# Projecting tiles 2 to 4 with split operands in a fused attention and recurrent-gate kernel

## The reference

```python
x = x + xattn(layernorm(x), ctx, ctx) @ W_proj.T + b_proj
def step(c, xt):                       # xt: rows of layernorm(x), 8 steps
    f = sigmoid(xt @ wf.T + c @ uf.T + bf)
    i = sigmoid(xt @ wi.T + c @ ui.T + bi)
    g = tanh(xt @ wc.T + c @ uc.T + bc)
    return f * c + i * g
h = tanh(layernorm(x) @ wo.T + c_final @ uo.T + bo)
return x + h
```

## Time and profile before

| | |
|---|---|
| median of three runs | 939.13 us (938.74 to 941.21) |
| profiled execution, its own time | 940.45 us |
| its span, first to last instruction | 938.5 us |
| PE busy | 920.8 us, 98% |
| DVE busy | 673.8 us, 72% |
| ACT busy | 476.1 us, 51% |
| POOL busy | 206.1 us, 22% |
| granted clock of PE | 1.000 of full speed |

### The profile page before, as it was taken

How to read it: one execution, slowest core, us unless ns; L and a number is a source line. 1 busy time by engine, 2 the same in 40 slices (tenths; PEclk the granted TensorE clock), 3 DMA queues, 4 the chain that set the end, 5 groups by cost and what they waited for, 6 DMA issues and landing times.

```text
span 938.5 us, 21983 instructions
## 1 busy us (share of the span) xinstructions
PE 920.8 (98%) x7842; PEld 716.7 (76%) x7842; DVE 673.8 (72%) x2275; ACT 476.1 (51%) x1430; POOL 206.1 (22%) x236
## 2 busy tenths in 40 slices
PE   8999899999999999999999999999999999999998
PEld 5555567678877788887877888788877888888887
DVE  6888898888779977997799878987798531143222
ACT  6888666655555544554465555555655421131222
POOL 4575322211110111111111111111101100003444
PEclk9999999999999999999999999999999999999999
DMA  9564223224443543444544444434333150049862
GB/s 299 167 191 154 86 80 109 73 82 130 132 130 116 133 131 94 139 111 126 129 141 116 117 114 123 114 108 110 98 98 92 50 164 0 1 175 383 317 235 101
DMA packets 139348, 123.58 MB, mean 132 GB/s; under 512 B 46824, under 2 KB 104168, under 8 KB 137704
## 3 DMA queue, kind: packets, MB, share of 16 engines
q1 hardware_dynamic: 138520, 121.91, 42.7%
q10 hardware_dynamic: 720, 0.27, 0.2%
HBM read 87.70 MB, written 34.46 MB: 130 GB/s over the span
## 4 chain that ended last, share of the span: by engine, by line
PE 87%; DVE 6%; issue 3%; ACT 2%; DMA 1%; POOL 0%; SPq 0%; DVEq 0%; POOLq 0%; ACTq 0%
PE ps_g L699 18%; PE ps_g L701 17%; PE ps_g L700 17%; PE ps_a L746 5%; PE ps_a L768 5%; PE ps_m L699 3%; PE ps_v L789 3%; PE ps_m L701 3%; PE ps_m L700 3%; PE ps_m L821 2%; PE ps_a L701 2%; PE ps_a L700 2%; PE ps_a L699 2%; DVE probs L1028 2%; PE ps_v L794 2%
## 5 line engine op out<-in xcount | busy, mean ns | idle before, releaser
L916 ACT ACTIVATE probs<-probs,rowmin 128x192 f32<-128x192 f32 (+1 forms) x512 | 239.4, 470 | 114.2 <-DVE rowmin L1028 114.2
L1028 DVE CUSTOM_DVE_ANT_0 probs<-ps_a,mask 128x192 f32<-128x192 f32 (+1 forms) x512 | 166.0, 385 | 30.2 <-PE ps_a L746 29.4
L699 PE MATMUL ps_g<-state_hi,gate_w 128*128 128x512 f32 x336 | 133.6, 398 | 0.0
L701 PE MATMUL ps_g<-state_hi,gate_w 128*128 128x512 f32 x336 | 131.1, 390 | 0.0
L700 PE MATMUL ps_g<-state_lo,gate_w 128*128 128x512 f32 x336 | 130.9, 389 | 0.0
L1063 DVE STREAM_TRANSPOSE keys<-probs 32x128 f32<-32x128 f32 x420 | 125.6, 299 | 5.6 <-issue 0.3
L963 ACT ACTIVATE gate<-ps_g,bias 128x512 f32<-128x512 f32 x84 | 57.6, 686 | 105.4 <-PE ps_g L701 104.8
L916 ACT ACTIVATION_READ_ACCUMULATOR probs<-probs,rowmin 128x1 f32 x512 | 96.3, 188 | 0.0
L678 POOL TENSOR_TENSOR attn_lo<-recip,attn_hi 128x512 fp32r<-128x512 f32 x23 | 29.7, 1293 | 276.4 <-ACT attn_hi L929 276.4
L921 ACT ACTIVATE probs_t<-ps_a 128x512 f32<-128x512 f32 x108 | 59.3, 595 | 50.9 <-PE ps_a L768 50.9
L699 PE MATMUL ps_g<-x2t_even,gate_w 128*128 128x512 f32 x192 | 80.0, 417 | 0.0
(11 more groups left out here) (220 smaller groups left out, 1724.9 us busy)
## 6 DMA issues: line engine op xcount, KB each, us to landing
values<-ctx_rows SPq DMA_DIRECT2D x34, 256.0 KB, 4.4
xr<-x SPq DMA_DIRECT2D x32, 256.0 KB, 3.5
keys<-ctx_t SPq DMA_DIRECT2D x16, 512.0 KB, 4.3
x_dram<-xr SPq DMA_DIRECT2D x32, 256.0 KB, 2.4
gate_w<-x2t_dram SPq DMA_DIRECT2D x8, 1024.0 KB, 9.7
keys<-ctx_t SPq DMA_DIRECT2D x16, 384.0 KB, 3.5
x2t_dram<-x2t_even SPq DMA_DIRECT2D x12, 512.0 KB, 4.1
x2t_dram<-x2t_odd SPq DMA_DIRECT2D x12, 512.0 KB, 4.4
```

What stands on the lines that cost most here:

```text
L699: pe.matmul(ps, lhs[0], rhs[0], start=start, stop=False)
L701: return pe.matmul(ps, lhs[1], rhs[0], start=False, stop=stop)
L916: act.activation(row, row, ACT.Exp, bias=rowmin[:, i % 2, h:h + 1], scale=-1.0, accum_out=rowsum[:, i // G % 2, i % G, h:h + 1]).then_inc( ...
L1028: dve.tensor_tensor_reduce(probs[:, i % 2, h, 0:SEEN[t]], ps_a[h][:, score_at[i]:score_at[i] + SEEN[t]], mask[:, MASK0[t]:MASK0[t] + SEEN[ ...
```

## The change

`WHOLE` becomes 2: tiles 2 to 4 are projected with split operands as well. Their steps `halves` are thereby in the list, at the end of slots 11, 15 and 19, right behind `mult`. The projections of tiles 2 and 3 stand behind the values of slots 12 and 16, where they stood in front; those of tiles 0 and 1 stay in front, and that of tile 4 was behind already. `split_proj` moves from slots 19 and 20 to slots 6 and 7. The waits that count from `WHOLE` (of `ln1b`, of `halves`, of the blend that overwrites `wp`) follow.

```diff
     FIRST_CELL = G * TT + 3
+    SPLIT_PROJ = G + 2
     OWN_BANKS = FIRST_CELL + 1
 
-    WHOLE = OWN_BANKS // G
+    WHOLE = 2
...
-        if s == 3 and i >= WHOLE:
+        if s == 3 and not early:
             tile_steps("mult", i)
-        if early:
+        if early and (s > 0 or i - 1 < WHOLE):
             tile_steps(("proj", "query", "turn2", "spread")[s], (i - 1, i + 1, i - 1, i)[s])
+        elif early:
+            pass
         elif n + 1 < SLOTS:
             steps.append(("exp", n + 1))
...
         if n in row_at:
             steps.append(("row", row_at[n]))
+        if early and s == 0 and i - 1 >= WHOLE:
+            tile_steps("proj", i - 1)
         gates()
...
-        if FIRST_CELL <= n < FIRST_CELL + 2:
-            steps.append(("split_proj", PAIR * (n - FIRST_CELL)))
+        if SPLIT_PROJ <= n < SPLIT_PROJ + 2:
+            steps.append(("split_proj", PAIR * (n - SPLIT_PROJ)))
```

## The result

The changed kernel takes 947.44 us (median of four runs, 945.92 to 948.40), the kernel before 940.17 beside it: ratio 1.0077, 95% interval 1.0063 to 1.0091. It is slower by 7.3 us, or 5.9 to 8.6. The forecast was 941.6 us with a range up to 944.2, so it had the direction right but not the size.

The account below looks back on a forecast made before the run. PE was taken to bound the early slots, ACT and DVE close behind. +0.5 (weights' split), +0.62, +0.62 and +0.75 (tiles 2 to 4) made +2.5 us: 942.95 profiled, 941.6 us as median, range 938.0 to 944.2.

Parts of the forecast that it names:

- The projection's own cost: PE, tiles 2 to 4: a split projection takes 2.86 us against 3.60 whole, 2.2 us less over three tiles.
- The chain of hand-overs: DVE's product through ACT's rounding and POOL's subtraction to PE: 2.22 us; net +0.62 us each for tiles 2 and 3.
- Tile 4: Slot 20: projection stays behind the values, its first product waits for the hand-overs; +0.75 us.
- The weights' split: Moved to slots 6 and 7: ACT copies delay PE by +0.5 us; removal from slots 19 and 20 gives nothing.
- ln1b: L1012 on DVE waits for POOL instead of the projection, about 1 us earlier for tile 4; gives nothing.
- the clock: PE's granted clock was taken to stay at 1.00 behind the new waits, as the trace showed around a 1.5 us gap.
- Rival D: New PE gaps lower its clock, three split projections take twice 2.86 us: +11.1 in all, 950.2 us; chance 0.02.
- Rival B: Hand-overs of tiles 2 to 4 are hidden, the whole projection saving stays: -1.7 us, 937.4 us; chance 0.15.
- E: Waits after slot 20 take up part of the delay: about +1 us, 940.1 us; chance 0.13.
- C: PE follows ACT in slots 6 to 11, copies cost their whole 2.1 us: sum +4.1, 943.2 us; chance 0.20.

Follow-up runs that it names:

- the filled kernel: Changed kernel with unused transposes filling PE's waits before the values of slots 12, 16, 24 and the scores of slot 22: 941.85 us, ratio 1.0020.
- halves behind: Changed kernel with the rounding of tiles 2 to 4 placed behind the next slot's turn on ACT and POOL: 944.87 us, ratio 1.0055.
- three places filled: Changed kernel with unused transposes before the values of slots 12 and 16 and the scores of slot 22: 943.10 us, ratio 1.0031.

## Why the prediction was wrong

**The projection's own cost** was right: 2.86 us in the stretches at full clock, slot 16 among them (79.76 to 82.61).

**The chain of hand-overs** was right in order and size. The product of tile 2 is followed by ACT and POOL as summed, with smaller gaps on the way: ACT 0.03 us behind DVE instead of 0.08.

```profile
58.18 0.66 DVE L1075 TENSOR_TENSOR tile_row<-ps_v,tile_row 128x512 f32<-128x512 f32 x1
```

```profile
58.87 0.63 ACT L934 ACTIVATE attn_hi<-tile_row 128x512 fp32r<-128x512 f32 x1 [1.43 <-DVE tile_row L1075]
59.41 0.58 ACT L926 ACTIVATE probs_t<-ps_g 128x512 f32<-128x512 f32 x1
...
97.97 0.63 ACT L934 ACTIVATE attn_hi<-tile_row 128x512 fp32r<-128x512 f32 x1 [3.82 <-DVE tile_row L1075]
98.51 0.58 ACT L926 ACTIVATE probs_t<-ps_a 128x512 f32<-128x512 f32 x1
```

```profile
59.58 1.28 POOL L683 TENSOR_TENSOR attn_lo<-tile_row,attn_hi 128x512 fp32r<-128x512 f32 x1 [0.96 <-ACT attn_hi L934]
...
78.34 1.27 POOL L683 TENSOR_TENSOR attn_lo<-tile_row,attn_hi 128x512 fp32r<-128x512 f32 x1 [0.76 <-ACT attn_hi L934]
```

58.84, where the product ends, to 61.01, the first split product, is 2.17 us against 2.22. At tile 3, where nothing but the chain holds PE, it is 2.17 us again, from 77.59 to 79.76, and the whole effect is +0.56 against +0.62, with no fall of the clock there; at tile 2 it is +0.66 once the wait is filled.

**Tile 4** was mis-placed. The forecast let PE wait before the values of slot 20, for 1.1 us more than the 1.53 that it waited there before. The scores of slot 22 stand in front of them in PE's queue and wait for the same copy (`turned_a`), as they write the bank that it reads. What is queued behind the rounding on ACT was named, but not everybody who waits for that. By itself this costs little, since the values would have waited next: 9.82 us with the gap filled, +0.98 against +0.75. But it made one wait of 3.19 us, the longest of the three, and the costliest fall stands behind it.

**The weights' split** was right: +0.54 us from slot 6 to 12 against +0.5, by the mechanism described; the kernel with only this edit shows +0.53 there, and +0.7 us in its median. Its removal from slots 19 and 20 gave nothing, as said.

**ln1b** was right as well: for tile 4 it starts at 61.88 us, 1.16 earlier than before, and nothing in PE's stretches is gained by it.

**The step that failed is the clock.** The sum took the waits at their length and put the clock behind them at nothing. Rival D named the mechanism, "the new gaps of PE lower its clock", but was given a chance of 0.02, because the trace of before showed a gap of 1.5 us at a clock of 1.00. That one row was no proof: in 15 of 33 other runs of the same kernel the clock read under 1.000. The measured price is 5.3 us (+7.0 on before for the changed kernel, +1.7 with its waits filled), in three falls of 1.3, 2.5 and 1.6 us instead of the +8.6 that D reckoned for three projections wholly at the lower clock. One of them came at tile 5, where the edit changed nothing but the moment; the forecast knew of no way in which a shift could cost. The Trainium skill ("TensorE: Matmul & The Clock Gate", section HAM oscillation) says that gaps in PE's work bring the gate back, and the runs bear it out here for gaps of 1.26 and 3.19 us, shorter than those of which that section speaks, and the very ones for which the forecast set it aside.

With the clock held by filling, the sum comes out: from slot 6 to the end of tile 5's projection the filled kernel takes 89.62 us and the one before 86.96, +2.7 against the +2.5 of the forecast. That its median, 941.85 us, lies beside the forecast of 941.6 is partly luck: the forecast added 2.5 us to a median of 939.13, and the measured difference is 1.7 us on 940.13.

Rival B is out: no hand-over was hidden. E had waits behind slot 20 take up some 1.5 us; behind tile 5's projection the changed kernel gives back 0.64 us and the filled one 0.48, for a reason that was not looked for, so E is right in a small part. C, PE following ACT through slots 6 to 11, is out with +0.54.

**What stays open** is when a given wait lowers the clock. The waits ahead of tile 5's projection, 0.36 and 1.20 us, are alike in all traces in which they aren't filled. With the projection starting at 119.53 (before), 120.16 (only the weights' split), 120.34 and 121.73 (only tile 4 split, filled and not), 123.91 (only slot 20 filled) and 124.16 us (only slots 12, 16 filled) the clock stays at 1.00; at 121.02 (halves behind), 121.29 (three places filled), 125.09 and 126.08 (changed, twice) it falls. So the length of the wait doesn't settle it. Something else has a part, the moment or what went before, and no experiment here controlled either. No kernel was found that beats the one before. A later place for the split projections was not tried: it would have to hide 2.2 us of hand-overs in slots where ACT and DVE are nearly as full as PE, for at most 2.2 us.

## What to carry to other kernels

Where PE runs at 98% and at full clock, a new wait on it has two prices, its length and what the clock costs behind it; in this kernel a wait of 1.2 to 3.2 us cost a further 1.3 to 2.5 us where the clock fell. A trace of before at clock 1.00 doesn't show that a wait is safe; the granted clock of several runs does, and dummy transposes in the wait tell the two prices apart with one more kernel. When a step is put into an in-order queue ahead of another, ask for all who wait for that other one, and which of them comes first in its own queue.

## What the runs showed of the hardware

A fall to half the clock lasted through 3.4 to 5.5 us of work here: at tile 2 the products came 0.43 us apart up to 63.70 and 0.23 apart from there, in the middle of an unbroken row of products. It occurred behind waits of 0.36 and 1.20 us ahead of tile 5's projection that in six other traces left the clock alone. And transposes whose result nobody reads, 0.12 us each, are enough to hold it: 22 of them in a wait of 3.2 us took 2.56 us of PE's time and saved about as much.
